# The softmax division of an attention block: per head pair in the attention stage, or per output tile in the last stage

## The reference, cut to what matters

```python
h = layernorm(x) * (1 + ca) + sa
q, k, v = h @ wq_w + wq_b, h @ wk_w + wk_b, h @ wv_w + wv_b
att = softmax(einsum('bqhfd,bkhd->bhfqk', q, k) / sqrt(32))   # over the keys
a = einsum('bhfqk,bkhd->bqhfd', att, v)
x = x + ga * (a @ wo_w + wo_b)
h = layernorm(x) * (1 + cb) + sb
logits = h @ router_w.T                       # 4 experts, the best 2 are kept
gates = softmax(top2(logits))
x = x + gb * sum_e gates[e] * (h @ A[e].T @ B[e].T) * 4
```

## Time and profile before

| what | value |
|---|---|
| median of 3 runs | 2838.37 us (2837.24 to 2840.28) |
| the profiled execution | 2836.98 us |
| its span, first to last instruction | 2835.2 us |
| busy: PE, DVE, ACT, POOL | 98%, 77%, 54%, 68% |
| attention stage | about 640 to 2340 us |
| last stage | about 2340 to 2835 us |

### The profile page before, as it was taken

How to read it: one execution, slowest core, us unless ns; L and a number is a source line. 1 busy time by engine, 2 the same in 40 slices (tenths; PEclk the granted TensorE clock), 3 DMA queues, 4 the chain that set the end, 5 groups by cost and what they waited for, 6 DMA issues and landing times.

```text
span 2835.2 us, 48789 instructions
## 1 busy us (share of the span) xinstructions
PE 2766.4 (98%) x14654; PEld 1698.5 (60%) x14654; DVE 2185.2 (77%) x2785; ACT 1520.1 (54%) x2915; POOL 1915.2 (68%) x710
## 2 busy tenths in 40 slices
PE   7999999999999999999999999999999999999998
PEld 4788888874444444444444444444444447888886
DVE  4433333358999999999999999999999968666675
ACT  3211111116766666666666666666667663445543
POOL 2433333318999999999999999999999986111110
PEclk9999999999999999999999999999999999999998
DMA  7544444434444443433444434433433443332331
GB/s 265 182 144 135 143 138 141 143 108 121 94 91 88 93 90 86 95 88 86 92 89 88 94 89 86 94 90 86 95 88 86 99 131 98 112 112 96 105 111 67
DMA packets 167567, 307.60 MB, mean 108 GB/s; under 512 B 49984, under 2 KB 91392, under 8 KB 159360
## 3 DMA queue, kind: packets, MB, share of 16 engines
q1 hardware_dynamic: 158352, 240.05, 29.1%
q0 software_dynamic: 9072, 66.06, 11.4%
HBM read 159.12 MB, written 79.82 MB: 84 GB/s over the span
## 4 chain that ended last, share of the span: by engine, by line
PE 69%; DVE 4%; issue 3%; ACT 1%; POOL 0%; DVEq 0%; ACTq 0%; POOLq 0%
PE back_ps L1304 20%; PE back_ps L1318 16%; PE s_ps L1278 15%; PE s_ps L1789 12%; PE back_ps L1838 2%; DVE mx L1195 2%; PE back_ps L1335 2%; PE back_ps L1810 1%; PE back_ps L1857 1%; ACT p_t L1178 1%; DVE wo_lo L1233 1%; DVE two_sum L1210 0%; PE back_ps L1293 0%; ACT h_t L1646 0%; PE s_ps L1367 0%
## 5 line engine op out<-in xcount | busy, mean ns | idle before, releaser
L1178 ACT ACTIVATE p_t<-back_ps 128x512 f32<-128x512 f32 x2048 | 1114.5, 596 | 479.2 <-PE back_ps L1304 411.9
L1195 DVE TENSOR_REDUCE mx<-s_ps 128x1 f32<-128x1024 f32 x1002 | 1173.1, 1209 | 110.2 <-PE s_ps L1278 101.0
L1102 POOL TENSOR_TENSOR p_sum<-p_sum,p_t 128x2048 f32<-128x2048 f32 x254 | 1165.5, 4588 | 46.2 <-ACT p_t L1178 29.9
L1304 PE MATMUL back_ps<-q_st,k_st 98*128 98x512 f32 x2048 | 814.7, 437 | 18.3 <-ACT p_t L1178 15.8
L1304 PEld LDWEIGHTS back_ps<-q_st,k_st 98*128 98x128 f32 x2048 | 345.4, 188 | 600.3 <-ACT p_t L1178 499.2
L1278 PE MATMUL s_ps<-k_st,q_st 96*128 96x512 f32 x2004 | 637.4, 397 | 6.8 <-DVE mx L1195 6.6
L1318 PE MATMUL back_ps<-p_t,v_sb 128*32 128x512 f32 x4096 | 548.1, 607 | 0.0
L1278 PEld LDWEIGHTS s_ps<-k_st,q_st 96*128 96x128 f32 x2004 | 379.0, 189 | 91.7 <-DVE mx L1195 23.2
L574 POOL TENSOR_TENSOR o_lo<-side,o_hi 128x512 fp32r<-128x512 f32 x80 | 104.1, 1302 | 321.0 <-ACT o_hi L544 320.8
L1102 POOL TENSOR_TENSOR p_sum<-p_t 128x2048 f32<-128x2048 f32 x64 | 313.1, 4893 | 10.4 <-ACT p_t L1178 10.4
L1210 DVE TENSOR_REDUCE two_sum<-p_t 128x512 f32<-128x1024 f32 x256 | 317.0, 1240 | 1.0 <-ACT p_t L1178 1.0
(11 more groups left out here) (151 smaller groups left out, 2904.6 us busy)
## 6 DMA issues: line engine op xcount, KB each, us to landing
p_sum<-two_sum POOLq DMA_DIRECT2D x63, 1024.0 KB, 6.9
q_st<-q_hi_d SPq DMA_DIRECT2D x128, 256.0 KB, 4.3
stage<-w_mod SPq DMA_DIRECT2D x48, 512.0 KB, 6.1
q_hi_d<-o_hi SPq DMA_DIRECT2D x64, 256.0 KB, 2.0
q_lo_d<-o_lo SPq DMA_DIRECT2D x64, 256.0 KB, 2.0
q_st<-q_lo_d SPq DMA_DIRECT2D x64, 256.0 KB, 4.1
att_d<-a_sb SPq DMA_DIRECT2D x128, 128.0 KB, 2.3
a_f<-att_d SPq DMA_DIRECT2D x32, 512.0 KB, 4.6
```

What stands on the lines that cost most here:

```text
L1102: nc.gpsimd.tensor_tensor(total, before, p_t[:, kt, :, :], ALU.add).then_inc(sum_done, 1)
L1178: nc.scalar.activation(p_t[:, s, c, :], st_ps[:, c % 2, :], ACT.Exp, scale=SCALE)\
L1195: nc.vector.tensor_reduce(mx[:, slot % 2, e:e + 1], s_ps[:, e % 2, :], AX_X, ALU.max)\
L1304: nc.tensor.matmul(st_ps[:, c % 2, :], k_st[:, slot // 2, s * P:(s + 1) * P], q_st[:, slot, jj, h * QW:(h + 1) * QW], start=True, stop=True)\
```

## The change

Attention no longer divides. ACT's copy of the numerators goes straight to DRAM (`num_d`). DVE copies the denominators out of PSUM (`take_den`), and SP stores two rows of 2 KB each of the two blocks (`den_d`), reads them back spread over 128 partitions x 16, DVE inverts these in place (`invert`), and SP stores them (`rden_d`). A pair's copy, inversion and last store lie one pair apart. There is one `rden` buffer in SBUF, so a pair's denominators are read back only when the inverses of the pair before have been stored.

In the last stage each tile has a second input, `r_f`: for every 32 partitions the inverse of their head, 128 tokens, 8 blocks. Four DMAs of 128 KB load it, each a row repeated over 32 partitions. There is one `r_f`. POOL multiplies `a_f` by `r_f` in place (128 x 1024) and counts `a_div_done`; ACT's `a_hi` waits for that in place of the load. Tiles 0 and 1 are multiplied during pairs 61 and 62.

```diff
@@ attend, sync @@
         def store(pair, par):
-            sp.wait_ge(a_ready, pair + 1)
+            sp.wait_ge(num_taken, pair + 1)
             for h in range(NQW):
-                sp.dma_start(att_d..., a_sb[...]).then_inc(a_out[par], 16)
+                sp.dma_start(num_d..., num_sb[...]).then_inc(num_out[par], 16)
+            for h in range(NQW):
+                if h == 0:
+                    sp.wait_ge(den_taken, pair + 1)
+                elif not below(pair, 2):
+                    sp.wait_ge(rden_out, pair * 16 - 16)
+                sp.dma_start(den_d[bass.ds(pair * HEADS, HEADS), h * QW:(h + 1) * QW],
+                             den_sb[h * HEADS * HD:(h + 1) * HEADS * HD:HD, par, :]).then_inc(den_out[par], 16)
+        def load_den(pair, par):
+            sp.wait_ge(den_out[par], (pair - par) * (8 * NQW) + 16 * NQW)
+            sp.dma_start(rden[:, :], spread(den_d, pair)).then_inc(den_back, 16)
+        def store_rden(pair):
+            sp.wait_ge(rden_done, pair + 1)
+            sp.dma_start(spread(rden_d, pair), rden[:, :]).then_inc(rden_out, 16)
...
-        store(NPAIR - 2, NPAIR % 2)
-        store(NPAIR - 1, (NPAIR - 1) % 2)
+        for pair in (NPAIR - 2, NPAIR - 1):
+            store_rden(pair - 2)
+            store(pair, pair % 2)
+            load_den(pair - 1, 1 - pair % 2)
+        store_rden(NPAIR - 2)
+        sp.wait_ge(rden_out, 16 * NPAIR - 16)
+        load_den(NPAIR - 1, (NPAIR - 1) % 2)
+        store_rden(NPAIR - 1)
@@ attend, vector @@
-        def divide(pair, piece):          # transpose, reciprocal 128x16, transpose back
+        def take_den(pair, par):
...
+            nc.vector.tensor_reduce(den_sb[:, par, :], den_ps.unsqueeze(2), AX_X, ALU.max).then_inc(den_taken, 1)
+        def invert(pair):
+            dve.wait_ge(den_back, pair * 16 + 16)
+            nc.vector.reciprocal(rden[:, :], rden[:, :]).then_inc(rden_done, 1)
...
         add_two(NPAIR - 1, REP - 1)
+        take_den(NPAIR - 2, NPAIR % 2)
+        invert(NPAIR - 3)
+        take_den(NPAIR - 1, (NPAIR - 1) % 2)
         for pair in (NPAIR - 2, NPAIR - 1):
-            for piece in range(3):
-                divide(pair, piece)
+            invert(pair)
@@ finish, sync @@
                 sp.dma_start(a_f[:, u, :, :], ...).then_inc(a_in[u], 16)
+                load_r(T, b, t)
                 sp.wait_ge(x1_ready, T - 3)
...
+        def load_r(T, b, t):
+            sp.wait_ge(a_div_done, T)
+            src = rden_d[bass.ds(b * (G * REP), G * REP), t * P:(t + 1) * P].rearrange("(k j) s -> j k s", j=REP)
+            for j in range(REP):
+                sp.dma_start(r_f[j * HD:(j + 1) * HD, :, :], src[j].partition_broadcast(HD)).then_inc(r_in, 16)
@@ finish, gpsimd @@
+                pool.wait_ge(a_in[u], (T - u) * 8 + 16)
+                pool.wait_ge(r_in, T * (16 * REP) + 16 * REP)
+                nc.gpsimd.tensor_tensor(a_f[:, u, :, :], a_f[:, u, :, :], r_f[:, :, :], ALU.mult).then_inc(a_div_done, 1)
                 pool.wait_ge(a_hi_done, T + 1)
@@ finish, scalar @@
-                act.wait_ge(a_in[u], (T - u) * 8 + 16)
+                act.wait_ge(a_div_done, T + 1)
                 act.wait_ge(o_ready, T * 2 - 2)
                 nc.scalar.copy(a_hi[u][:, :, :], a_f[:, u, :, :]).then_inc(a_hi_done, 1)
...
-                    act.wait_ge(meet.a_ready, att_d.shape[0] * 2)
+                    act.wait_ge(meet.rden_out, 16 * num_d.shape[0] * 2)
```

More of the change, by code:

```diff
@@ L55 @@
     a_f: Any
+    r_f: Any
     a_hi: Any
@@ L147, in at @@
             return nc.alloc_sbuf_tensor_at(name, shape, dt, offset=offset)
-        meet = Meet(at("a_f", [P, 2, KT, P], F32, q_at),
+        meet = Meet(at("a_f", [P, 2, KT, P], F32, q_at), r_f,
                     [at(f"a_hi{u}", [P, KT, P], F32R, q_at + (2 + 2 * u) * S * 4) for u in range(2)],
@@ L936, in attend @@
     num_taken = sem("num_taken")
-    den_taken = sem("den_taken")
-    rden_step = sem("rden_step")
-    a_ready = meet.a_ready
-    a_out = [sem(f"a_out{u}") for u in range(2)]
+    den_taken = meet.den_taken
+    num_out = [sem(f"num_out{u}") for u in range(2)]
+    den_out = [sem(f"den_out{u}") for u in range(2)]
+    den_back = sem("den_back")
+    rden_done = sem("rden_done")
+    rden_out = meet.rden_out
     def pairs(eng, do):
@@ L1033, in do @@
                   .then_inc(meet.up_in[0], 16)
-            if not (below(pair, 2) or is_int(pair, NPAIR - 1)):
+            if not below(pair, 4):
+                store_rden(pair - 4)
+            if not below(pair, 2):
                 store(pair - 2, slot % 2)
+            if not below(pair, 3):
+                load_den(pair - 3, 1 - slot % 2)
+            if is_int(pair, NPAIR - 2):
+                sp.wait_ge(meet.a_div_done, 1)
+                load_r(1)
             if not is_int(pair, NPAIR - 1):
@@ L1053, in do @@
                 sp.dma_start(meet.down[:, :, :], lora_in).then_inc(meet.down_in, 16)
-                store(pair - 2, slot % 2)
                 sp.wait_ge(two_done, NPAIR * REP)
@@ L1102, in do, with divide_tile @@
                 nc.gpsimd.tensor_tensor(total, before, p_t[:, kt, :, :], ALU.add).then_inc(sum_done, 1)
-                if kt == DIVIDE_AFTER and not below(pair, 2):
-                    divide(pair - 2, slot % 2)
-        def divide(pair, par):
-            pool.wait_ge(rden_step, pair * 2 + 2)
-            pool.wait_ge(num_taken, pair + 1)
-            if not below(pair, 2):
-                pool.wait_ge(a_out[par], (pair - par) * (8 * NQW))
-            nc.gpsimd.tensor_tensor(a_sb[:, par, :], rden[:, :], num_sb[:, par, :], ALU.mult).then_inc(a_ready, 1)
+                if kt == DIVIDE_AFTER:
+                    if is_int(pair, NPAIR - 3):
+                        divide_tile(0)
+                    if is_int(pair, NPAIR - 2):
+                        divide_tile(1)
+        def divide_tile(T):
+            pool.wait_ge(meet.a_in[T], 16)
+            pool.wait_ge(meet.r_in, 16 * REP * (T + 1))
+            nc.gpsimd.tensor_tensor(meet.a_f[:, T, :, :], meet.a_f[:, T, :, :], meet.r_f[:, :, :], ALU.mult)\
+              .then_inc(meet.a_div_done, 1)
         pairs(pool, do)
@@ L1248, in do @@
                     add_two(pair, TWO_STEPS.index(s))
-                if s in DIVIDE_STEPS and not below(pair, 2):
-                    divide(pair - 2, DIVIDE_STEPS.index(s))
+                if s == DEN_STEP and not below(pair, 2):
+                    take_den(pair - 2, slot % 2)
+                if s == RDEN_STEP and not below(pair, 3):
+                    invert(pair - 3)
                 for item in beside(pair, slot, s):
@@ L1445, in sem @@
         return ctx.enter_context(nc.semaphore(name))
-    a_f, a_hi, a_lo, x_sb, bo, ga = meet.a_f, meet.a_hi, meet.a_lo, meet.x_sb, meet.bo, meet.ga
+    a_f, r_f, a_hi, a_lo, x_sb, bo, ga = meet.a_f, meet.r_f, meet.a_hi, meet.a_lo, meet.x_sb, meet.bo, meet.ga
     mod_rows, down, up_w, up_f, up_hi = meet.mod_rows, meet.down, meet.up_w, meet.up_f, meet.up_hi
@@ L1553, in do @@
             now = tile_of(slot, b, t, 0)
+            if is_int(slot, 3):
+                load_r(3, 0, 3)
             if now and not (isinstance(now[0], int) and now[0] < 4):
```

90 lines of the change are left out of this document (50 added, 40 removed).

## The result

The kernel with the change takes 2938.41 us (median of 4 runs, 2931.58 to 2944.49) against 2839.32 us (4 runs, 2837.24 to 2841.45) on the same chip: 1.0346 times as long, 95% interval 1.0324 to 1.0368. It is slower, as forecast, but by 99 us and not by 25; 2938 lies far outside the range of 2841 to 2892. The profiled execution took 2940.29 us, its span is 2938.2.

The account below looks back on a forecast made before the run. PE was busy 98% of the span, exchanging work with ACT in attention; waits of PE or ACT were taken to decide. 2837 + 0 (pairs) + 12 (passage) + 13 (slots) = 2862 us, range 2841 to 2892.

Parts of the forecast that it names:

- the landing of `r_f` in the slot: Last-stage slot: r_f was taken to land at 2613.2 us, 7.87 us after the late addition ends.
- the forecast of the passage: Between attention and last stage: +12 us from a late start, slots 3 to 5 and clock; bounds 0 and +20.
- Repeating pairs, 0: Attention's repeating pairs: work taken from DVE and POOL lies beside the PE and ACT exchange, so 0 us change.
- the case "faster": Attention rival: PE's wait for the maxima vanishes, 25 us in 64 pairs, 2824 us in all; chance 0.07.
- Pairs 61 and 62, "POOL is idle for more than that": End of attention: products of tiles 0 and 1, 2.38 us in place of 1.45, fit POOL's idle time; 0 us.
- The chain of five landings: Passage: alternating small loads and stores take 11.6 to 14.1 us, ending near 2354; DVE starts the last stage 10 us late.
- The 1.7 us for the clock: Passage: 1.7 us on TensorE's clock if the longer wait brings one more 3.4 us stretch at half of it.
- The slot: Last stage: a loop through four engines closes at 15.3 us against 14.8, +0.5 us a slot, +13 us over 26.
- The factor of 1.45: Last-stage slot: slowdown assumed for r_f's repeated source over a_f's 1.84 us landing interval, giving a landing at 2613.2.
- The rival of dear slots: Last stage: r_f lands at 2614 or later, product and a_hi slip whole, +46 us, 2895 us; chance 0.16.
- The port: DVE and GpSimd share one port pair, first holds it; POOL's products block DVE's additions whole; 0.3 us counted per slot.
- The low end drawn from a page: Last-stage slots: no price named for a repeated source, so the slots would cost nothing and the sum be 2849 us.

Follow-up runs that it names:

- 1: Changed kernel without the four r_f loads for tiles 3 to 31, products kept on old inverses: 2866.36 us, ratio 1.0094.
- 2: Changed kernel with neither r_f loads nor products for tiles 3 to 31, a_hi waiting for a_f alone: 2860.43 us, ratio 1.0074.
- 12: Version with reordered r_f, moved products, reordered transfers and separate last inverse buffers, without loads and products from tile 3 on: 2850.69 us, ratio 1.0045.
- 5: Changed kernel with the next tile's four r_f loads issued at slot end, ahead of the out store; whole computation: 2878.75 us, ratio 1.0138.
- 7 to 11: On 5, cumulatively: products moved, chain ahead of bulk, pair 61 bulk later, own inverse buffers; last, on 5 alone, tiny products: 2877.07, 2869.29, 2870.59, 2867.07, 2870.56 us.
- 3: Changed kernel with the four r_f loads for tiles 3 to 31 reading each partition from rows of its own: 2895.08 us, ratio 1.0197.
- 6: Kernel before, plus four repeated-row loads of 128 KB per slot from tile 4 on into a buffer nobody reads: 2852.18 us, ratio 1.0049.
- 4: Changed kernel with r_f for tiles 3 to 31 loaded by one 512 KB transfer from rows of its own: 2882.51 us, ratio 1.0159.

## Why the prediction was wrong

The step that failed is the landing of `r_f` in the slot, 7.87 us behind the late addition in the forecast. It was 9.64 us in the slot shown and came to some 10.4 in the mean, and the slots took 2.7 us more, not 0.5. The runs give this account of the 99 us: the loads of `r_f` 72.0 (changed kernel less 1), the products from tile 3 on 5.9 (1 less 2), order and place of small transfers, bulk and products in pairs 61 to 63 9.7 (2 less 12), and 12 for the rest of attention and passage. The two middle terms are of the size that pair 61 alone varies by between executions of one attention (27.4 to 36.8 us), so they are not settled; the 72.0 is clear of that. That 12 is also the forecast of the passage is chance: the passage of the changed kernel cost 24.8 us (16.0 and 8.8).

- **Repeating pairs, 0:** right. PE's waits for the maxima fell, and a pair did not; the case "faster" fell with it.
- **Pairs 61 and 62, "POOL is idle for more than that": wrong for pair 61.** The idle time stands ahead of the last additions, the product ahead of earlier ones. Pair 61 took 7.7 us more and pair 62 nothing. I had asked whether POOL has room and not who is queued behind the product, nor what SP issues ahead of the denominators.
- **The chain of five landings:** its length was nearly right (10.5 us against 11.6 to 14.1), its start mis-sized: near 2341 in the forecast, 2361.5 in fact. SP reached `ga` 16 us later than before, and I let the 8 KB behind it land with `ga`'s 8.8 us where they took 13.7. DVE was 28 us late and not 10; 16.0 of these are of the passage, 7.7 of pair 61 and 4.4 not of the change. PE's wait ahead of its first transposes was forecast at about 11 us and came to 15.90. The 3 us for slots 3 to 5 were small beside the 5.4 to 5.9 of 1 less 2. The 1.7 us for the clock, one more stretch of 3.4 us at half of it, is the size of the stretch before (2357.3 to 2360.7 us); 33 us in place of 7 came, and no run shows what they cost.
- **The slot: the loop was right, its terms too small.** This is the failed step. 4.66 us from `a_hi` to the end of the late addition were 4.64. But from the late addition to the product there were 9.64 us where I had 7.87 + 0.3, the product took 2.71 in place of 2.38. In the third batch `r_f` came later still: its median landing was 6.7 us, in the batches beside it 5.3 and 5.2. The traces of 5 and of 7 to 11 have long slots in that batch too. Why is open; neither loads from rows of their own (3) nor repeated rows of `att_d` (6) show it. The factor of 1.45 was taken between two loads elsewhere in the kernel, while these ran behind `out` and `a_f`, and the time of four issues (2.31 us) was left out. By 3 and 4 the repetition was worth 43 us and the transfers' number 12.6, or in the steady slots all that was left (15.8 to 14.9 us). Neither the place behind `out` and `a_f` (4) nor the traffic (6) lengthens a steady slot by itself.
- **The rival of dear slots** (2895 us, 0.16) had the mechanism that came, with a bound of 1.8 us a slot that was no bound.
- **The port.** DVE's 7.21 us, starting 0.2 us behind POOL's product, and its 0.78 us in 3, starting 0.2 us ahead of it, show it: the first to start goes through, the other waits. The rule that I had weighed, the Trainium skill, "SBUF — State Buffer", "SBUF: two separate sides", agrees; I had applied it to the slots, where it cost little (the steady slots of 1 and 2 are equal), and not to pair 61.
- **The low end drawn from a page** did not hold: the same loads in 512-byte pieces, from rows of their own and from rows repeated over 32 partitions, differ by 43 us (3). By the Trainium skill, "DMA: Bandwidth & Descriptors", "Specifications", both are at the smallest piece for line rate; that section gives no price for a repeated source, and I had read this as none.

## What to carry to other kernels

When a step that had slack gets a second input, work out the landing of that input in its own queue (place, number of issues, what runs ahead), not from a free one; once the slack is used up the loop closes, and each microsecond of landing is one of time in every slot. Here one plain load of 512 KB stayed within the slack and four of 128 KB did not. Where the load can be issued a step ahead for nothing, do that before anything else: here it gave back 60 of 99 us. Before bulk goes into a queue, look which small transfers behind it an engine waits for. And a mean over slots or a single trace can mislead: look at the intervals one by one, and compare one and the same stretch in several executions. None of these versions beats the kernel before: the best whole computation took 2867 us.
